# Attention of the routed rows: the null value is taken off the value rows and put back as a bias, and heads are turned and weighed in pairs

## The reference, cut to what matters

```python
def _heavy_attn(xq, ctx, scores_kv, gamma, q_w, kv_w, null_kv, out_w, rope_q, rope_k):
    xq, ctx = _rmsnorm(xq, gamma), _rmsnorm(ctx, gamma)
    q = (xq @ q_w)...                                   # 8 heads of 64
    kv = jnp.einsum('hdi,bni->bhnd', kv_w, ctx)
    k, v = (kv[..., :dh], kv[..., dh:])
    v = v * scores_kv[:, None, :, None]
    q, k = _apply_rope(rope_q[:, None], q), _apply_rope(rope_k[:, None], k)
    k = jnp.concatenate([nk, k], axis=2)                # one null key ahead of the 256
    v = jnp.concatenate([nv, v], axis=2)                # one null value
    attn = jax.nn.softmax(jnp.einsum('bhid,bhjd->bhij', q, k) * dh ** (-0.5), axis=-1)
    out = jnp.einsum('bhij,bhjd->bhid', attn, v)
    return out... @ out_w
```

## Time and profile before

| | us |
|---|---|
| median of 3 runs | 4278.78 (4276.99 to 4278.88) |
| profiled execution, whole | 4281.28 |
| its span, first to last instruction | 4279.5 |
| TensorE busy | 3615.6 (84% of the span) |
| VectorE busy | 2516.2 (59%) |
| ScalarE busy | 1937.2 (45%) |
| GpSimd busy | 1495.2 (35%) |
| mean granted TensorE clock | 0.914 |

### The profile page before, as it was taken

The page is one execution under the profiler, slowest core; times in us unless marked ns, Lnnn a source line. Parts: engine busy times, 40 slices in busy tenths (PEclk is TensorE's granted clock), DMA queues, the critical chain, the costliest instruction groups (busy, mean ns, idle before and its releaser), DMA issues. The chain is left out here.

```text
span 4279.5 us, 88934 instructions
## 1 busy us (share of the span) xinstructions
PE 3615.6 (84%) x34025; PEld 2029.8 (47%) x34025; DVE 2516.2 (59%) x6732; ACT 1937.2 (45%) x4521; POOL 1495.2 (35%) x1807
## 2 busy tenths in 40 slices
PE   6378789987799879997899878998799988998787
PEld 2245444554446544464445543465444644455444
DVE  6754757366563666546573666636674565736652
ACT  5123435555264443554355442554445443545433
POOL 4233441254323441234422533234512444235311
PEclk9589899998899889998899988999899988999888
DMA  6210230002300221002300023002310023001220
GB/s 233 70 33 13 57 102 19 13 27 52 98 17 22 53 75 48 15 12 61 103 15 21 22 50 96 17 22 53 93 31 15 12 61 103 15 24 30 50 62 6
DMA packets 230803, 205.73 MB, mean 48 GB/s; under 512 B 11458, under 2 KB 212418, under 8 KB 230347
## 3 DMA queue, kind: packets, MB, share of 16 engines
q1 hardware_dynamic: 226338, 190.51, 15.9%
q0 software_dynamic: 3328, 8.39, 0.7%
q10 hardware_dynamic: 720, 1.15, 0.1%
HBM read 121.73 MB, written 77.69 MB: 47 GB/s over the span
## 5 line engine op out<-in xcount | busy, mean ns | idle before, releaser
L2343 ACT ACTIVATE arena<-pb 128x512 f32<-128x512 f32 (+3 forms) x1536 | 674.3, 491 | 308.4 <-PE pb L1577 299.5
L2423 POOL TENSOR_TENSOR arena<-arena,small 128x512 f32<-128x512 f32 x256 | 288.6, 1129 | 465.9 <-DVE small L1753 464.5
L1536 PE MATMUL pb<-arena 96*32 96x128 bf16 (+3 forms) x6912 | 385.5, 297 | 72.0 <-DVE arena L2022 30.8
L2172 ACT ACTIVATE arena<-arena,small 128x256 f32<-128x256 f32 x512 | 256.0, 500 | 395.8 <-DVE small L1736 389.8
L2587 POOL TENSOR_SCALAR_AFFINE_SELECT arena<-arena 128x256 f32<-128x256 f32 x512 | 221.2, 435 | 524.0 <-ACT arena L2343 522.9
L1577 PE MATMUL pb<-arena 98*32 98x512 bf16 (+3 forms) x4608 | 389.9, 344 | 10.9 <-ACT arena L2343 7.0
L1595 PE MATMUL pb<-arena,v 128*17 128x512 f32 (+3 forms) x3072 | 370.8, 504 | 30.5 <-POOL arena L2587 21.9
L2027 DVE TENSOR_REDUCE arena<-pb 128x1 f32<-128x512 f32 x512 | 331.4, 684 | 83.8 <-PE pb L1536 82.0
L1736 DVE CUSTOM_DVE_ANT_0 arena<-pb,wmask 128x256 f32<-128x256 f32 x512 | 195.7, 419 | 220.7 <-PE pb L1288 220.6
L1536 PEld LDWEIGHTS pb<-arena 96*32 96x32 bf16 x6912 | 165.9, 102 | 290.5 <-DVE arena L2022 78.0
L1288 PE MATMUL pb<-arena 128*128 128x256 f32 x1024 | 279.8, 398 | 5.4 <-issue 4.0
(11 more groups left out here) (336 smaller groups left out, 7253.7 us busy)
## 6 DMA issues: line engine op xcount, KB each, us to landing
arena<-split_q SPq DMA_DIRECT2D x64, 384.0 KB, 4.2
arena<-split_k SPq DMA_DIRECT2D x24, 768.0 KB, 6.6
split_q<-arena SPq DMA_DIRECT2D x64, 192.0 KB, 2.3
split_q<-arena SPq DMA_DIRECT2D x96, 128.0 KB, 2.0
split_k<-arena SPq DMA_DIRECT2D x64, 192.0 KB, 2.4
split_k<-arena SPq DMA_DIRECT2D x96, 128.0 KB, 2.1
arena<-split_k SPq DMA_DIRECT2D x24, 384.0 KB, 5.7
xn<-h_d SPq DMA_DIRECT2D x8, 1024.0 KB
```

The lines of the kernel that those rows point to most:

```text
L1536: mm = t.matmul(out[r:r + 32], qh[:, q0 + r:q0 + r + 32], keys, **kw)
L2172: ins = s.activation(pm[n % 3][:, j], sm[n % 2][:, j], ACT.Exp, bias=nmx[:, 2 * sl + j:2 * sl + j + 1], scale=-1.0, accum_out=sml[:, 2 * s ...
L2343: s.activation(pp[pn % 4][:, h % 2, 0:w_], bank[n % 3][:, 0:w_], ACT.Exp).then_inc(a_exp1, 1)
L2423: g.tensor_tensor(pm[n % 3], pm[n % 3], rcl[:, 2 * sl:2 * sl + 2].unsqueeze(2).broadcast_to([P, 2, 2 * P]), ALU.mult).then_inc(p_norm0, 1)
```

## The change

The null value leaves the product. It is loaded on all 128 partitions (`nullv_b`, kept in the last quarter of `hqk` until the second half of the keys is written there), and subtracted from the value rows as these are taken from PSUM. `nullv`, now with head dimensions on partitions, is added as the bias of ScalarE's copy to `otT`. So the null column needs no transpose, no copy and no product.

Values are projected first (steps j = 0), into banks 7 and 6; queries and keys follow one double step later than before. Pieces are turned in pairs: four transposes fill bank 6, one VectorE copy of 512 columns takes them, and the pair is weighed in one go, both heads for the first 128 keys and then both for the second, so that the 32-column products of the pair lie on four column tiles. The ring `ph` has 6 places in place of 4, `pth` has one place of four blocks in place of two of three. The projection with `who` moves half a step ahead. SyncE issues one more DMA per batch, at the start of the stage, which waits for the splits of the batch before.

```diff
-nullv_nmr = sb("nullv_nmr", [P, HD])
-nullv = nullv_nmr[0:1, :].rearrange("p (h d) -> p h d", d=DH)
-nmr = [nullv_nmr[64:64 + 2 * G1, i * NH // 2:(i + 1) * NH // 2].bitcast(BF16) for i in range(2)]
+nullv = sb("nullv", [P, H0 // 2])
+nmr_w = sb("nmr", [P, HD])
+nmr = [nmr_w[64:64 + 2 * G1, i * NH // 2:(i + 1) * NH // 2].bitcast(BF16) for i in range(2)]
...
+nullv_b = hqk[:, 3]
...
-ph = [view([NQ + 4])[:, 0:NQ + 1] for _ in range(4)]
-pth = [view([3, P]) for _ in range(2)]
+ph = [view([NQ + 1]) for _ in range(6)]
+pth = view([4, P])
...
+        if j == 0:
+            for half_ in range(2):
+                bk = 7 - half_
+                for w in left[bk]:
+                    t.wait_ge(*w)
+                t.wait_ge(a_nT, 2 * b + 2)
+                for k in range(KD):
+                    mm = tiled(t.matmul, 32, bank[bk], nT[:, 1, k, half_ * P:(half_ + 1) * P], whv[:, k, :], start=k == 0, stop=k == KD - 1)
+                mm.then_inc(t_hp, 1)
+                left[bk] = [(v_vh, 2 * b + half_ + 1)]
+                yield
+        elif j < 5:
+            w_ = (whq, whq, whk, whk)[j - 1]
+            src, half_ = (j - 1) // 2, (j - 1) % 2
+            for w in left[7]:
+                t.wait_ge(*w)
+            for k in range(KD):
+                mm = tiled(t.matmul, 32, bank[7], nT[:, src, k, half_ * P:(half_ + 1) * P], w_[:, k, :], start=k == 0, stop=k == KD - 1)
+            mm.then_inc(t_hp, 1)
+            left[7] = [(a_hqk, 4 * b + j)]
+            yield
+            if j >= 2:
+                turn_qk(j - 2)
+            yield
+        else:
+            turn_qk(3)
+            yield
+            yield
...
-    def head_turn(n):
+    def pair_turn(m):
         for w in left[6]:
             t.wait_ge(*w)
-        t.wait_ge(p_hn, 16 * b + n + 1)
-        for c, (lo, wd) in enumerate(((1, P), (1 + P, P), (0, 1))):
-            mm = t.transpose(bank[6][0:wd, c * P:(c + 1) * P], ph[n % 4][:, lo:lo + wd], ident[:, :])
+        for h in range(2):
+            n = 2 * m + h
+            t.wait_ge(p_hn, 16 * b + n + 1)
+            for c in range(2):
+                mm = t.transpose(bank[6][:, (2 * h + c) * P:(2 * h + c + 1) * P], ph[n % 6][:, 1 + c * P:1 + (c + 1) * P], ident[:, :])
         mm.then_inc(t_hturn, 1)
-        left[6] = [(v_hpt, 16 * b + n + 1)]
-
-    def head_weigh(n):
-        half_, h = divmod(n, H0)
-        ob = bank[6][(h % 2) * DH:(h % 2 + 1) * DH, 3 * P:4 * P]
+        left[6] = [(v_hpt, 8 * b + m + 1)]
+
+    def pair_weigh(m):
         for w in left[6]:
             t.wait_ge(*w)
-        t.wait_ge(v_hpt, 16 * b + n + 1)
         t.wait_ge(v_vh, 2 * b + 2)
         for c in range(2):
-            tiled(t.matmul, 32, ob, vh[:, c, h, :], pth[n % 2][:, c], start=c == 0, stop=False, skip_group_check=True)
-        tiled(t.matmul, 32, ob, nullv[0:1, h, :], pth[n % 2][0:1, 2], start=False, stop=True, skip_group_check=True).then_inc(t_hpv, 1)
-        if h % 2:
-            left[6] = [(a_ho, 8 * b + n // 2 + 1)]
+            for h in range(2):
+                mm = tiled(t.matmul, 32, bank[6][h * DH:(h + 1) * DH, 0:P], vh[:, c, (2 * m + h) % H0, :], pth[:, 2 * h + c],
+                           start=c == 0, stop=c == 1, skip_group_check=True)
+        mm.then_inc(t_hpv, 1)
+        left[6] = [(a_ho, 8 * b + m + 1)]
...
         if n < 2 * H0:
             head_scores(n)
-        if 0 <= n - 3 < 2 * H0:
-            head_turn(n - 3)
-        yield
-        if 0 <= n - 4 < 2 * H0:
-            head_weigh(n - 4)
         if n in (H0 + 4, 2 * H0 + 4):
             head_project(n // H0 - 1)
+        yield
+        if n % 2 == 0 and 0 <= n - 4 < 2 * H0:
+            pair_turn((n - 4) // 2)
+        if n % 2 and 0 <= n - 5 < 2 * H0:
+            pair_weigh((n - 5) // 2)
         yield
...
+    def value_rows(half_):
+        v.wait_ge(t_hp, 6 * b + half_ + 1)
+        v.wait_ge(nullv_in, 16 * (b + 1))
+        v.scalar_tensor_tensor(out=vh[:, half_].rearrange("p h d -> p (h d)"), in0=bank[7 - half_], scalar=sc_all[:, 4 * b + 2 + half_:4 * b + 3 + half_],
+                               in1=nullv_b, op0=ALU.mult, op1=ALU.subtract).then_inc(v_vh, 1)
...
+        if j == 1:
+            value_rows(1)
+        yield
+        if j == 0:
+            value_rows(0)
+        elif j < 5:
+            rope(j - 1)
...
-    def head_turn(n):
-        v.wait_ge(t_hturn, 16 * b + n + 1)
-        if b or n >= 2:
-            v.wait_ge(t_hpv, 16 * b + n - 1)
-        v.tensor_copy(pth[n % 2][:, 0:2], bank[6][:, 0:2 * P].rearrange("p (c q) -> p c q", q=P))
-        v.tensor_copy(pth[n % 2][0:1, 2], bank[6][0:1, 2 * P:3 * P]).then_inc(v_hpt, 1)
+    def pair_turn(m):
+        v.wait_ge(t_hturn, 8 * b + m + 1)
+        if b or m:
+            v.wait_ge(t_hpv, 8 * b + m)
+        v.tensor_copy(pth[:, :, :], bank[6].rearrange("p (c q) -> p c q", q=P)).then_inc(v_hpt, 1)
...
+        if 1 <= j < 5:
+            s.wait_ge(t_hp, 6 * b + j + 2)
             s.wait_ge(v_hss, 5 * b + 5)
-            s.activation(hqk[:, j], bank[7], ACT.Copy, scale=DH ** -0.5 if j < 2 else 1.0).then_inc(a_hqk, 1)
-        if 1 <= j < 5:
-            turn_qk(j - 1)
+            if j == 4:
+                s.wait_ge(v_vh, 2 * b + 2)
+            s.activation(hqk[:, j - 1], bank[7], ACT.Copy, scale=DH ** -0.5 if j < 3 else 1.0).then_inc(a_hqk, 1)
+        if j >= 2:
+            turn_qk(j - 2)
...
-        if n >= 4:
-            s.wait_ge(t_hturn, 16 * b + n - 3)
+        if n >= 6:
+            s.wait_ge(t_hturn, 8 * b + (n - 6) // 2 + 1)
         if b or n >= 4:
             s.wait_ge(v_hrc, 16 * b + n - 3)
         exp_tables()
-        s.activation(ph[sl], bank[7][:, 0:NQ + 1], ACT.Exp, bias=mxh[:, n:n + 1], accum_out=smh[:, sl:sl + 1]).then_inc(a_hexp, 1)
+        s.activation(ph[n % 6], bank[7][:, 0:NQ + 1], ACT.Exp, bias=mxh[:, n:n + 1], accum_out=smh[:, sl:sl + 1]).then_inc(a_hexp, 1)
+
+    def pair_weigh(m):
+        s.wait_ge(t_hpv, 8 * b + m + 1)
+        if m >= 4:
+            s.wait_ge(t_ho, 2 * b + 1)
+        s.activation(otT[:, m % 4], bank[6][:, 0:P], ACT.Identity, bias=nullv[:, m % 4:m % 4 + 1]).then_inc(a_ho, 1)
...
-        g.tensor_tensor(ph[sl], ph[sl], rch[:, sl:sl + 1].broadcast_to([P, NQ + 1]), ALU.mult).then_inc(p_hn, 1)
+        g.tensor_tensor(ph[n % 6][:, 1:NQ + 1], ph[n % 6][:, 1:NQ + 1], rch[:, sl:sl + 1].broadcast_to([P, NQ]), ALU.mult).then_inc(p_hn, 1)
...
+    if b:
+        sp.wait_ge(split_out[1][1], 16 * SPLIT_DMAS * b)
+        sp.wait_ge(t_hqkT, 4 * b)
+    sp.dma_start(nullv_b, a["null_v"].partition_broadcast(P)).then_inc(nullv_in, 16)
```

88 lines of the change are left out of this document (30 added, 58 removed).

## The result

The kernel after takes 4229.97 us (median of 4 runs, 4228.27 to 4234.26) against 4278.83 for the kernel before: 0.989 of it, 95% interval 0.9878 to 0.9902, or 49 us less. 4204 was predicted. The profiled execution took 4230.35 us, its span is 4228.6, and the mean granted clock is 0.912 (0.914 before).

What follows compares the result with a forecast made beforehand. TensorE's time was taken as the kernel's while pieces run: 63.5 us from batches 1 to 7, plus 16.3 in batch 0, less 4 in the projections, makes 75.8 off 4281.28; 2.5 less for the median, rounded to 4204, range 4167 to 4250.

Steps and rivals of the forecast that it cites:

- The price of a pair: TensorE's turning and weighing of two pieces: 1.25 us in place of 2.76, 1.51 less, 12.1 a batch.
- The fixed part f: Fixed cost of one TensorE visit, 0.12 us beside 0.11 a round, split from the weighing's 0.56 and null product's 0.34.
- I take a quarter lost: Pieces of batches 1 to 7: a quarter of 12.1 us a batch lost to exposed chains, leaving 63.5 us gained.
- Batch 0: Its pieces gain 16.3 us: 12.1 off TensorE plus 5.8 of null-row copy waits, less 1.6 of waits left.
- The projections: Ahead of the pieces: 1.6 us new wait at the last keys' turn against 1.1 gone; 0.5 lost a batch, 4 in all.
- VectorE and the load: Pair copy 0.686 us, value row with subtraction 0.75; SyncE's 256 KB load in 5 to 6 us, hidden by 2.
- nothing either way: ScalarE's bias on the copy to `otT`, and GpSimd's one column fewer: no effect, both engines over 35% free.
- The four tiles do not run together: Rival, chance 0.10: no overlap of column tiles at 128 columns, 1.04 us saved a pair; 52 us gained, 4227.
- The chains take over: Rival, chance 0.17: ring of turn, copy, weighing and ScalarE copy through `pth` and bank 6 binds; 40% kept, 40 us, 4239.
- nothing turned slower: Clock rival: thinner TensorE work keeps pieces at 1.2 GHz; 4343 with 40 us more a batch; chance 0.05 including late DMA.
- The signs I had named: Profile after: weighing 0.56 to 0.70 us, pieces 104 to 107; wrong if weighing nears 1.1 or clock falls below 0.93.
- Idle time grows by over 6 us: Sign of a wrong forecast: TensorE's idle time in the pieces of a batch grows by over 6 us.

Runs made afterwards that it cites:

- weighing twice: Against the kernel after: each pair's eight weighing products issued twice into the same place; 4249.5 us, ratio to before 0.9935.
- the old order: Against the kernel after: queries and keys projected first, values last, null subtraction from the value rows and its load left out; 4221.2 us, 0.9876 of before.
- the probe: Against the kernel after: one more 32x128 ScalarE copy behind each piece's exponential, 128 in all; 4251.8 us, 0.9939 of before.
- the late copies: Against the kernel after with scores of pieces 1 and 3 in bank 6 and values last (4180.7 us): copy and bias of pairs 3 to 7 on VectorE; 4191.7 us.

## Why the prediction was right and wrong

**Right**: the sign, and the range (4167 to 4250). The time was 26 us off, outside the forecast's own narrower range (4188 to 4222), and most of it is one term.

**The price of a pair** held in sum and not in its parts. Weighing I put at 0.65; it takes 0.44 beside the light attention and 0.55 to 0.58 in batch 0. The turns came to 0.62 for 0.60. Per pair 1.66 us left TensorE, where 1.51 was forecast. The fixed part f = 0.12 of a visit was taken from rows of batch 0, where another tiling always follows: the null product with its one contraction row behind the weighing, and tiles of 64 columns behind the null product. Where a visit on the same column tiles follows it is not paid, and that took another 1.8 us a batch off the scores, which I had not seen. With it 15.0 us were removed and not 12.1, so the forecast would have been further off with the right price.

**"I take a quarter lost"** is the mis-sized term. 63.5 us were forecast for batches 1 to 7 and 41.7 arrived, 22 of the 26 us that are missing. Of 15.0 us, 60% were lost. The quarter was an average over pieces of two kinds: where TensorE's time counts in full (pieces 4 to 9) 30% was lost, close to the guess; in the last six, with five of the eight pairs, 77%. The earlier trace rows gave one busy share for 114 us, 97%, and I took it as one regime. The share did not tell the stretches apart: it was 44.40 of 45 and 60.27 of 62 in the two parts.

```profile
1169.00:1214.00 45.00, 44.40 (x733) 20.32 (x733) 35.70 (x85) 30.14 (x69) 7.74 (x17) 0.97 0.11 29
1214.00:1276.00 62.00, 60.27 (x946) 28.78 (x944) 37.04 (x108) 39.16 (x97) 16.47 (x33) 1.00 0.02 5
```

(The kernel before.) Other engines are at 63% or below in the last part, and still it gave back. In the kernel after the same two parts read:

```profile
1149.50:1190.00 40.50, 39.92 (x703) 19.26 (x704) 32.94 (x73) 29.25 (x69) 7.64 (x16) 0.93 0.12 32
1190.00:1251.00 61.00, 55.92 (x902) 26.89 (x891) 36.41 (x97) 39.29 (x98) 16.79 (x33) 1.00 0.02 5
```

Now 5.1 us of 61 are idle in the last part. Before, the null products and the extra visits had lain in these gaps between the light attention's own steps, and cost little: weighing twice shows it from the other side, with 2.2 us put in for 0.3.

**Batch 0**: 16.3 forecast, 18.1 measured in the pieces; the 0.5 lost ahead of them belongs to the projections. The waits for the copy fell from 5.8 us to 0.7, below the 1.6 I had allowed.

**The projections**: -4 forecast, -6.3 in the traces; the old order gives all of it back, 8 us in the traces. The mechanism was the one named, the turn of the last keys without two value projections as cover, at the place that I named. Its size was 0.8 a batch in place of 0.5.

**VectorE and the load**: 0.690 us for the pair's copy (0.686 forecast), 0.742 for a value row (0.75), and the load's 256 KB land in 4.2 us (5 to 6 forecast), never waited for:

```profile
arena<-in_null_v SPq DMA_DIRECT2D x8, 256.0 KB, 4.2
```

**ScalarE's bias, "nothing either way"**: the instruction went from 281 to 375 ns. The Trainium skill (ScalarE: Activation LUTs, What ACT_TABLE_LOAD costs) gives 93 ns more for a bias that is read as an operand; the trace agrees with 94, and I had not looked it up. 64 x 0.094 is 6 us of ScalarE. By the probe's 22 us for 39.5 that would be an estimated 3 us of time; the late copies gave no sign that work in this place costs as much as the probe's. It was not measured apart.

**The rivals.** "The four tiles do not run together" gave 4227, within 3 us of the result, and is false: the visit takes 0.44 us, not 1.1. That its number came is luck. "The chains take over" had the right kind of cause and the wrong chain: I had looked at the ring of `pth` and bank 6, and TensorE waits 2 us for it in the whole span. The chains that came out are the light attention's own. The clock in the pieces fell from 0.96 to 0.95, not below 0.93, and nothing turned slower.

**The signs I had named** were too mild. "Idle time grows by over 6 us" did not happen (3.3 to 8.8 us), nor did the clock fall below 0.93, and yet the pieces took 111 us and not 104 to 107. Of TensorE's busy time in batch 2 8.5 us went and not 12, although 15.0 a batch were removed by the starts: the same matmuls of the light attention stand further apart and still count as busy, since their ends are modelled. And the weighing stood outside its own sign, 0.56 to 0.70, on the good side, which said nothing about the time. Starts would have been the better sign.

**Open**: which instruction sets the pace of the last six pieces. A microsecond more costs there 0.1 on TensorE, 0.3 on VectorE and 1.0 on ScalarE behind an exponential, and one less of the pair's copy on ScalarE costs or brings nothing. An earlier start of the light attention's exponentials by itself was not tried.

## What to carry to other kernels

Before a saving on the busiest engine is counted, split the stretch by its partners: ask at each place which other work runs beside it, and whether that has gaps in which the removed work lay. A busy share of 97% says nothing about it where ends are modelled; a kernel that adds a known cost at each place does, and here it told 1.0 from 0.1 us per microsecond in one run. When each piece waits a little for the piece ahead at the start of a stage, look at the granted clock of the next 20 us: a second bank for the first pieces was worth half as much as the whole change, and more. And moving a cost from one engine to another cannot tell which of them is the limit, since both may be.

## What the hardware showed that I had not expected

- The same 16 records of 128 columns take 0.44 us from start to start where work on column tiles of 32 follows and 0.55 to 0.58 where the whole array or tiles of 64 do; scores of 257 columns 0.44 and 0.54. What stands behind a visit sets its price.
- One visit of scores per batch placed in another bank gave 23 us in before and 28 in after: of before's 2.8 us a batch, 2.4 came in pieces 0 to 3, where the granted clock rose from 0.61 to 0.82, and 0.7 in pieces 4 to 9; the rest gave 0.3 back.
- A ScalarE copy of 0.31 us behind each exponential cost 0.23 us a piece where TensorE was 99% busy and ScalarE 72%, 0.32 in the last six pieces, and nothing in batch 0.
